# Second cross-attention: where between the units of maxima a finished batch's softmax denominators are spread and divided

## The reference

```python
kv = (mem @ W_kv).reshape(B, Nkv, 2, HEADS, HEAD_DIM)
q = (x @ W_q).reshape(B, Nq, HEADS, HEAD_DIM).transpose(0, 2, 1, 3)
attn = jnp.einsum('bhqd,bhkd->bhqk', q, k) * SCALE
attn = jax.nn.softmax(attn, axis=-1)
out = jnp.einsum('bhqk,bhkd->bhqd', attn, v)
return out @ W_proj + b_proj
```

## Time and profile before

| | |
|---|---|
| median of 3 runs | 3010.06 us (3008.7 to 3012.23) |
| the profiled execution, its own time | 3012.54 us |
| its span, first to last instruction | 3010.8 us |
| mean granted TensorE clock | 0.926 |
| TensorE busy | 2581.7 us, 86% |
| VectorE busy | 1556.6 us, 52% |
| ScalarE busy | 1401.3 us, 47% |
| GpSimd busy | 905.7 us, 30% |
| stage B's units of maxima | the first reduction starts at 692.3 us, the last at 2410.7 us |

### The profile page before, as it was taken

One profiled execution on the slowest core, in us unless ns is written; L12 is line 12 of the kernel. 1 busy time (PEld: TensorE's weight loads), 2 busy tenths in 40 slices (PEclk: granted clock), 3 DMA queues, 4 the chain that ended last, 5 costly groups with the idle time before them and its releaser, 6 DMA issues.

```text
span 3010.8 us, 75851 instructions
## 1 busy us (share of the span) xinstructions
PE 2581.7 (86%) x32176; PEld 2161.8 (72%) x32180; DVE 1556.6 (52%) x2693; ACT 1401.3 (47%) x2563; POOL 905.7 (30%) x868
## 2 busy tenths in 40 slices
PE   6999823247999999999999999999999973799997
PEld 3555511137888888888888888888888742699997
DVE  3434377733446445455455455454554623477775
ACT  1212111124565565555656656656656431455564
POOL 1000023344433433442442443443433203211121
PEclk9999955569999999999999999999999965899999
DMA  8888600031010110110100101101101002566665
GB/s 331 328 313 317 238 0 0 0 110 45 24 46 24 35 35 23 35 35 23 39 31 24 46 24 35 35 23 35 34 24 35 2 1 102 169 200 215 202 203 152
DMA packets 48582, 270.21 MB, mean 90 GB/s; under 512 B 4896, under 2 KB 23584, under 8 KB 33696
## 3 DMA queue, kind: packets, MB, share of 16 engines
q1 hardware_dynamic: 40160, 255.82, 23.4%
q0 software_dynamic: 8160, 10.29, 2.2%
HBM read 247.58 MB, written 20.61 MB: 89 GB/s over the span
## 4 chain that ended last, share of the span: by engine, by line
issue 40%; PE 27%; POOL 20%; DVE 6%; DMA 3%; ACT 3%; POOLq 1%; SPq 0%; DVEq 0%; ACTq 0%
POOL k_lo L539 7%; POOL ctx_lo L547 6%; PE PS L1035 3%; PE PS L1015 3%; PE PS L1380 2%; PE PS L1381 2%; PE PS L1382 2%; POOL qbd_lo L552 2%; DMA unit_raw<-in_experts 1%; PE PS L1302 1%; POOL sideB L566 1%; PE PS L1397 1%; PE PS L1399 1%; PE PS L1398 1%; PE PS L1163 1%
## 5 line engine op out<-in xcount | busy, mean ns | idle before, releaser
L1649 DVE TENSOR_REDUCE mpart<-PS 128x1 f32<-128x802 f32 (+1 forms) x512 | 488.0, 988 | 443.1 <-PE PS L1151 442.9
L835 ACT ACTIVATE probs<-PS 128x1024 f32<-128x1024 f32 (+1 forms) x416 | 425.5, 1023 | 228.2 <-PE PS L1302 223.6
L539 POOL TENSOR_TENSOR k_lo<-sideB,k_hi 128x400 fp32r<-128x400 f32 (+1 forms) x256 | 255.7, 999 | 354.4 <-ACT k_hi L771 354.0
L547 POOL TENSOR_TENSOR ctx_lo<-ctx_raw,ctx_hi 128x801 fp32r<-128x801 f32 x128 | 224.8, 1765 | 431.9 <-ACT ctx_hi L783 431.9
L1302 PE MATMUL PS<-qbd_hi,k_hi 64*128 64x256 f32 (+1 forms) x1664 | 313.4, 372 | 0.0
L1151 PE MATMUL PS<-k_hi,qbd_hi 128*128 128x512 f32 (+2 forms) x1024 | 263.0, 359 | 22.7 <-POOL ctx_lo L547 13.6
L1163 PE MATMUL PS<-probs,vals 128*32 128x64 f32 x13312 | 272.9, 222 | 3.6 <-ACT probs L835 3.5
L770 ACT COPY sideB<-PS 128x400 f32<-128x400 f32 (+1 forms) x256 | 126.6, 494 | 274.4 <-PE PS L1131 274.4
L1163 PEld LDWEIGHTS PS<-probs,vals 128*32 128x32 f32 x13312 | 205.3, 110 | 66.7 <-ACT probs L835 15.5
L1138 PE MATMUL PS<-wkv_hi,ctx_hi 128*128 128x256 f32 (+1 forms) x832 | 236.4, 284 | 0.0
L1302 PE MATMUL PS<-qbd_hi,k_lo 64*128 64x256 f32 (+1 forms) x1664 | 235.0, 278 | 0.0
(11 more groups left out here) (325 smaller groups left out, 6134.0 us busy)
## 6 DMA issues: line engine op xcount, KB each, us to landing
unit_raw<-in_experts SPq DMA_DIRECT2D x46, 1536.0 KB, 7.1
ctxN<-in_ctxN SPq DMA_DIRECT2D x16, 3328.0 KB, 10.9
ctxT<-in_ctxT SPq DMA_DIRECT2D x16, 3204.0 KB, 10.5
ctx_raw<-in_ctxT SPq DMA_DIRECT2D x64, 801.0 KB, 4.4
slots_d<-pad_rows SPq DMA_DIRECT2D x2, 2990.0 KB, 18.4
xg<-slots_d SPq DMA_DIRECT2D x23, 260.0 KB, 2.8
x<-in_x SPq DMA_DIRECT2D x1, 2048.0 KB, 10.2
sum_d<-x SPq DMA_DIRECT2D x1, 2048.0 KB, 6.3
```

Source lines behind the costliest of these rows:

```text
L539: g.tensor_tensor(k_lo[:, n, a, c:c + width], k_raw[p % 2][:, 0:width], k_hi[:, n, a, c:c + width].bitcast(F32), ALU.subtract).then_inc(s. ...
L547: g.tensor_tensor(ctx_lo[:, a, cols], ctx_raw[:, cols], ctx_hi[:, a, cols].bitcast(F32), ALU.subtract).then_inc(s.ctx_lo_ready, 1)
L835: act.activation(probs[rows, t % PROBS, :], PS[rows, 1024 * (t % 2):1024 * (t % 2) + 1024], ACT.Exp).then_inc(s.pr_ready, 1)
L1649: v.tensor_reduce(mpart[:, pair, half:half + 1], PS[:, at:at + width], AX, ALU.max).then_inc(s.mx_red, 1)
```

## The change

Both `end_batch` calls, TensorE's and VectorE's, move from behind the third unit of maxima (u = 2) to behind the fifth (u = 4). No instruction is added or taken away, and nothing else moves. On TensorE the two matmuls of L1174 now stand between unit 4 and the fourth piece of keys (of the eight), where they stood between unit 2 and the second piece. On VectorE the reciprocal and the product stand between the reductions of units 4 and 5 in place of those of units 2 and 3.

```diff
@@ -1273,7 +1273,7 @@
                     if not (first and n == 0):
                         if u == 0:
                             weigh(1 - n, KEY_TILES - 1)
-                        if u == 2:
+                        if u == 4:
                             end_batch(1 - n, not first)
                     if ahead and u in PIECE_AFTER:
                         project(pieces.pop(0), 1 - n)
@@ -1647,7 +1647,7 @@
                     at = 1024 * ((u + 1) % 2)
                     v.wait_ge(s.mx_ps, T["mx"].up())
                     v.tensor_reduce(mpart[:, pair, half:half + 1], PS[:, at:at + width], AX, ALU.max).then_inc(s.mx_red, 1)
-                    if u == 2 and not (first and b == 0):
+                    if u == 4 and not (first and b == 0):
                         end_batch(1 - b)
```

## The result

The changed kernel takes 3021.08 us (median of 7 runs, 3020.26 to 3024.89) against 3010.06 us before. The ratio is 1.0041, 95% interval 1.0031 to 1.0051: 12 us slower (9 to 15). The forecast was 3003.8, and the range ended at 3010.

What follows compares the result with a forecast made beforehand. TensorE was taken to bound batches 1 to 30. Waits of 0.6 and 0.42 go, 0.7 and 0.1 of restart come: 0.21 a batch, 6.2 us over 30, giving 3003.8 us; range 2999 to 3010.

Steps and rivals of the forecast that it cites:

- The wait for the sums goes, 0.6 a batch: On TensorE, the spreading product L1174 no longer waits for ScalarE's copy of the sums: 0.6 us a batch gone.
- A new wait stands before unit 7: On TensorE, unit 7 waits 0.7 us for unit 5's late reduction; unit 9's old wait of 0.42 goes.
- The detour's 3.02, the 1.03 of release and the 0.47 after a wait: Walk's steps: 3.02 us between reductions around VectorE's detour; unit 1.03 after reduction two units before; piece 0.47 after waiting unit.
- Without a wait the product would cost between 0.53 and 0.7; I take 0.62: On TensorE, the assumed cost in us of the spreading product L1174 when it need not wait for the sums.
- The exact price of the spreading product doesn't enter: it lies in the shadow of the new wait: On TensorE, L1174's cost was said not to affect the 0.2 us gained a batch, being hidden by unit 7's wait.
- A start 0.01 behind GpSimd's still won: Argument against rival 2: in an earlier stage, VectorE's L1473 started 0.01 us from GpSimd's operation and took its 0.75.
- Rival 2: GpSimd's k_lo starts before VectorE's multiplication L1639 and holds it 0.8 us: 17.5 us slower, 3027.6 us; chance 0.08.
- the growing L1639: Sign of a wrong prediction: VectorE's multiplication L1639 takes longer than its usual 0.42 us in the profile after.
- The Trainium skill's rule of the shared port: VectorE with two SBUF inputs and GpSimd reading SBUF share ports; a lost race was taken as a full block.
- That VectorE is the engine whose chain decides: VectorE's chain of reductions and detour was said to decide everything in the 0.2 us gained a batch.

Runs made afterwards that it cites:

- GpSimd later: Changed kernel plus two one-column ScalarE copies before the fourth piece's rounding, delaying GpSimd's k_lo, both SBUF inputs kept: 3002.49 us, ratio 0.9978 to before.
- The place behind unit 3 without the hold: Kernel before with both calls moved behind unit 3 and the multiplication reading the sums from PSUM: 2984.92 us, ratio 0.9915.
- VectorE's part alone: Kernel before with only VectorE's reciprocal and multiplication moved behind unit 4, TensorE's spreading product still behind unit 2: 3042.05 us, ratio 1.0108.

## Why the prediction was wrong, point by point

- *The wait for the sums goes, 0.6 a batch*: right in kind. No such wait is left, and unit 3 starts 1.83 behind unit 1 (1519.53 to 1521.36) where it was 3.04. The 1.21 between them are the wait and the product together. I divided them as 0.6 and 0.62; the kernel that copies the sums earlier shows 0.79 for the wait.
- *A new wait stands before unit 7, since unit 5's reduction comes late; unit 9's wait goes*: right in kind. Forecast 0.7, counted from the start that unit 7 could have had; so counted it is 1.54 (1526.18 + 0.365 to 1528.08; 1.37 by the row). The hold of the multiplication is 0.63 of the difference, and 0.18 is that unit 7 was ready sooner, since the product was cheaper.
- *The detour's 3.02, the 1.03 of release and the 0.47 after a wait*: right. Where the multiplication isn't held (the PSUM source behind unit 4) unit 10 starts at 11.32 as against 11.31 in the walk (1513.09 to 1524.395), and the time is 3002.34 as against 3003.8.
- *"Without a wait the product would cost between 0.53 and 0.7; I take 0.62"*: **this term was mis-sized.** From unit 4 to unit 5 there are 1.90 (1522.81 to 1524.71), of which a unit and a piece take 1.465, so the product costs **0.435**; with the sums copied earlier it costs 0.42 (1508.97 to 1510.49, less a piece's 1.10). The row of before held 0.1 of restart after its wait, such as the earlier trace rows show for the units behind a wait (0.47 against 0.365), and I took that for a part of the product and put another 0.1 on top.
- *"The exact price of the spreading product doesn't enter: it lies in the shadow of the new wait"*: **this is the step that failed.** On TensorE it lay in the shadow. But the product also stands in front of the fourth piece, and by way of ScalarE it sets when GpSimd starts. Being 0.18 cheaper, it brought `k_lo` forward: to 6.42 behind unit 1 (1519.53 to 1525.95), where I had reckoned 6.53 to 6.70. The multiplication came at 6.54, reckoned 6.52. So `k_lo` was first by 0.12, where I had it second by 0.0 to 0.2.
- *"A start 0.01 behind GpSimd's still won"*: no margin to build on. To the nanosecond the two starts in the earlier trace rows lie 0.001 apart, and 0.001 to 0.003 in all 24 such pairs of that stage; the row's two decimals make 0.01 of it. There VectorE did win: GpSimd's operation took 1.31, and 0.77 in this row of before, where no VectorE operation with two SBUF inputs ran beside it:

```profile
394.91 0.77 POOL L518 TENSOR_SCALAR work<-work,convw,convb 128x512 f32<-128x512 f32 x1
```

In the kernel with GpSimd later, the multiplication started 0.009 and 0.014 behind (batches 30 and 1) and was held for 0.74. Whether the tie lies between 0.003 and 0.009 for every pair of operations, or differs from pair to pair, is open. The rival was said to need a lead of some tenth of a us; 0.01 is enough. Rival 2 was drawn up with the right mechanism, and given 0.08, because the product's lower bound, 0.53, was read from a row behind a wait, and the tie from a rounded one.
- *Rival 2's price, 0.8 and 3027.6*: too high, though the growing L1639 is the sign that I had named for being wrong. With a lead of 0.12, GpSimd's operation had already run part of its 0.89, and the hold is 0.63. The loss of 0.43 a batch gives 3023 by the same sum, against 3021.08.
- *The Trainium skill's rule of the shared port ("SBUF — State Buffer", "SBUF: two separate sides")*: whichever starts first holds it for its whole instruction and the other blocks; the runs agree, with 0.42 for the multiplication when first and 0.98 to 1.17 when second by up to 0.19. The hold ended 0.14 before the recorded end of GpSimd's operation, so "whole" isn't the recorded duration. They agree as well with its condition that VectorE's operation have two SBUF inputs: with one, neither engine is held (0.42, and 0.89 for `k_lo`).
- *That VectorE is the engine whose chain decides*: right, and it has a second side. Of the 24 us that the wait for the sums cost, its removal alone gives 10. The place behind unit 3 without the hold keeps it: the 0.79 and unit 9's 0.42 go, unit 7's new wait of 0.34 and its 0.1 of restart come, and unit 10 starts 0.78 sooner (26 us by the ratio).

On VectorE's side the hold goes by its second SBUF input and not by its write: with the sums from PSUM the multiplication still writes `attn4` to SBUF, and isn't held. What stays open is GpSimd's side: whether its two reads or its write are what holds VectorE up, no run here tells apart.

## What to carry to other kernels

When an operation that shares something with another engine is moved, work out the start of its new neighbour on that engine as carefully as its own, and trust no margin of 0.1 us: the sign of this change hung on 0.12. Don't take an operation's cost from a row behind a wait: part of the wait's price is in it. A wait that is removed is worth what the next one in line leaves of it, so walk the streams to where they meet again. Where one input of an elementwise operation still lies in PSUM, reading it there can take the operation out of such a race at no cost.

## What the runs showed of the hardware

The hold has a sharp end. Counted from the start of GpSimd's operation of 0.89 us, the multiplication was let go at the same moment, however late it came:

| kernel | multiplication starts behind `k_lo` | it takes | held (less 0.425) | sum |
|---|---|---|---|---|
| GpSimd later, batch 1 | 0.01 | 1.17 | 0.74 | 0.75 |
| changed kernel, loop | 0.12 | 1.05 | 0.63 | 0.75 |
| changed kernel, batches 1 and 30 | 0.19 | 0.98 | 0.56 | 0.75 |
| VectorE's part alone | 0.55 | 0.63 | 0.20 | 0.75 |
| sums copied earlier | 0.74 | 0.44 | 0.01 | 0.75 |
| GpSimd later, loop | -0.06 | 0.42 | 0 | |

So it ends some 0.14 before GpSimd's recorded end. That is a block and not a sharing, the third possibility named with the kernel that has GpSimd later: GpSimd's operation stays at its 0.89 to 0.90, and each 0.01 that VectorE comes later is 0.01 less of hold. The turn from nothing to the full hold lies between a start 0.06 ahead and one 0.01 behind. The hold is part of the recorded duration of VectorE's operation and shows as no wait of its own; only the longer operation gives it away.
